# Scattering two sorted edge tables straight from the full index array, with the pieces of the first table divided anew over three stages

## The kernel before, in words

| phase | table | rounds | issued by |
|---|---|---|---|
| dst_in | src | 1 | L393 |
| dst_hist | src | 3 | L446 |
| dst_rank | src | 9 | L564 |
| proj0 | src | the rest, 4 | L1992 |
| up0 | dst | 3 | L1995 |
| proj1 | dst | the rest, 14 | L2017 |

## Time and profile before

### The profile page before, as it was taken

How to read it: one execution, slowest core, us unless ns; L and a number is a source line. 1 busy time by engine, 2 the same in 40 slices (tenths; PEclk the granted TensorE clock), 3 DMA queues, 4 the chain that set the end, 5 groups by cost and what they waited for, 6 DMA issues and landing times. The chain is left out here.

```text
span 6893.5 us, 55872 instructions
## 1 busy us (share of the span) xinstructions
PE 3674.6 (53%) x14811; PEld 2847.0 (41%) x14811; DVE 3431.6 (50%) x6662; ACT 1000.6 (15%) x2079; POOL 3392.8 (49%) x3358
## 2 busy tenths in 40 slices
PE   1373256662001455554666666685666659764542
PEld 1263155551001344443344444674454448333331
DVE  7594344443000444556677777446777762222225
ACT  0000122211000111111211111332111113210000
POOL 4787766668886455550254453004454410037662
PEclk9655567766555577776788887897888879886666
DMA  1142233441100233332455554115555530233333
GB/s 38 28 101 41 46 113 113 117 87 30 18 2 8 82 94 94 94 88 55 148 158 154 155 159 111 42 51 163 151 163 152 154 78 13 104 122 93 93 91 55
DMA packets 289794, 630.52 MB, mean 91 GB/s; under 512 B 79692, under 2 KB 134320, under 8 KB 286384
## 3 DMA queue, kind: packets, MB, share of 16 engines
q0 software_dynamic: 168256, 437.11, 25.6%
q1 hardware_dynamic: 121328, 190.89, 8.6%
HBM read 560.35 MB, written 66.48 MB: 91 GB/s over the span
## 5 line engine op out<-in xcount | busy, mean ns | idle before, releaser
L862 PE MATMUL edge_sums<-edge_rows,edge_hot 128*128 128x272 f32 (+3 forms) x4640 | 1518.4, 491 | 896.2 <-issue 241.3
L809 POOL DMA_INDIRECT edge_rows<-kv_rows,dst_index x928 | 879.8, 948 | 1547.7 <-POOLq L89 668.1
L862 PEld LDWEIGHTS edge_sums<-edge_rows,edge_hot 128*128 128x128 f32 x4640 | 1112.6, 248 | 1207.7 <-issue 411.1
L809 POOL DMA_INDIRECT edge_rows<-rel_rows,dst_other_index x464 | 466.4, 1005 | 755.3 <-ACTq L89 565.2
L1102 PE MATMUL edge_own_rows<-dst_x,edge_hot_t 128*128 x1856 | 615.6, 490 | 163.2 <-DVE edge_rows L936 118.4
L809 POOL DMA_INDIRECT edge_rows<-xl_rows,dst_index x464 | 457.9, 987 | 464.3 <-PE edge_sums L862 249.0
L809 POOL DMA_INDIRECT edge_rows<-rows,src_index x464 | 454.1, 979 | 235.5 <-issue 127.3
L1102 PEld LDWEIGHTS edge_own_rows<-dst_x,edge_hot_t 128*128 128x128 f32 x1856 | 442.6, 248 | 301.0 <-issue 220.5
L211 POOL DMA_INDIRECT table_dst<-proj_dst_put_stage x350 | 418.4, 1195 | 97.8 <-issue 86.2
L1019 DVE TENSOR_TENSOR edge_rows<-edge_rows,edge_turn_p 128x2048 f32<-128x2048 f32 x174 | 396.6, 2280 | 119.1 <-ACT edge_rows L1181 119.0
L872 DVE TENSOR_TENSOR l_acc<-l_acc,edge_sums 128x258 f32 (+1 forms) x464 | 197.9, 427 | 496.0 <-PE edge_sums L862 212.6
(11 more groups left out here) (389 smaller groups left out, 5386.5 us busy)
## 6 DMA issues: line engine op xcount, KB each, us to landing
edge_where<-local_dst SPq DMA_DIRECT2D x174, 256.0 KB
dst_rank_keys<-in_dst SPq DMA_DIRECT2D x85, 312.5 KB
rel_rows<-proj_out SPq DMA_DIRECT2D x25, 1024.0 KB
edge_where<-local_src SPq DMA_DIRECT2D x58, 256.0 KB
edge_rows<-kv_rows,dst_index POOLq DMA_INDIRECT x928
kv_rows<-proj_out SPq DMA_DIRECT2D x50, 260.0 KB, 2.0
edge_rows<-rows,src_index POOLq DMA_INDIRECT x464
edge_rows<-xl_rows,dst_index POOLq DMA_INDIRECT x464
```

The lines of the kernel that those rows point to most:

```text
L809: pool.indirect_dma_start(out=self.rows[:, h * U + b, 0:self.width], out_offset=None, in_=self.source[:, :], in_offset=bass.IndirectOffset ...
L862: last = nc.tensor.matmul(sums[p % len(sums)][:, 0:width], self.hot[s % 2][:, 2 * (p % 4) + i, :], self.half(s)[:, 2 * (p % 4) + i, first: ...
```

## The change

The staging buffers, their copies and the semaphore `staged` go. `piece` writes all its DMAs out, without a hardware loop, and each reads slot numbers and data from `stage_all` itself. The waits on `put[u]` now stand before the five DMAs of a group and ask for the group five back. The unused argument `ready` goes, and `stage_all` loses its last five columns, which only the copy read. The source table's rounds are divided 1, 4, 10 and the rest (2) over `dst_in`, `dst_hist`, `dst_rank` and `proj0`; those of the other table stay 3 and 14.

```diff
     def __init__(self, hold, tag, table):
         self.tag, self.table, self.next = tag, table, 0
-        self.stage_all = hold.sb(f"{tag}_stage_all", [EP, ET + LOOK, 5], i32)
+        self.stage_all = hold.sb(f"{tag}_stage_all", [EP, ET, 5], i32)
 
-    def piece(self, nc, ph, pool, n, ready=None):
+    def piece(self, nc, ph, pool, n):
         n = min(n, self.ROUNDS - self.next)
         if n < 1:
             return
-        first, table, stage_all = self.next * SLOTS, self.table, self.stage_all
+        put = [ph.sem(f"{self.tag}_put{u}") for u in range(SLOTS)]
+        for i in range(n):
+            for u in range(SLOTS):
+                after(pool, put[u], i * 16 * LOOK)
+                for j in range(LOOK):
+                    t = (self.next + i) * SLOTS * LOOK + u * LOOK + j
+                    pool.indirect_dma_start(
+                        out=self.table[:, :], out_offset=bass.IndirectOffsetOnAxis(ap=self.stage_all[:, t, 0:1], axis=0),
+                        in_=self.stage_all[:, t, 1:5], in_offset=None).then_inc(put[u], 16)
         self.next += n
-        stage = ph.sb(self.tag + "_put_stage", [EP, SLOTS, LOOK, 5], i32)
-        staged = ph.sem(self.tag + "_put_staged")
-        put = [ph.sem(f"{self.tag}_put{u}") for u in range(SLOTS)]
-        if ready:
-            pool.wait_ge(ready, 1)
-        nc.gpsimd.tensor_copy(stage[:, 0, :, :], stage_all[:, first * LOOK:(first + 1) * LOOK, :]).then_inc(staged, 1)
-
-        def body(i):
-            for u in range(SLOTS):
-                g, v = i * SLOTS + u, (u + 1) % SLOTS
-
-                after(pool, put[v], (i + (1 if v == 0 else 0)) * 16 * LOOK)
-                pool.wait_ge(staged, g + 1)
-                if ready and v == 0:
-                    pool.wait_ge(ready, i + 2)
-                nc.gpsimd.tensor_copy(stage[:, v, :, :],
-                                      stage_all[:, bass.ds((g + first + 1) * LOOK, LOOK), :]).then_inc(staged, 1)
-                for j in range(LOOK):
-                    pool.indirect_dma_start(
-                        out=table[:, :], out_offset=bass.IndirectOffsetOnAxis(ap=stage[:, u, j, 0:1], axis=0),
-                        in_=stage[:, u, j, 1:5], in_offset=None).then_inc(put[u], 16)
-
-        rounds(pool, n, body)
         for u in range(SLOTS):
             pool.wait_ge(put[u], n * 16 * LOOK)
...
-                scatter_beside(nc, ph, block, (earlier, 3))
+                scatter_beside(nc, ph, block, (earlier, 4))
...
-            scatter_beside(nc, ph, block, (earlier, 9))
+            scatter_beside(nc, ph, block, (earlier, 10))
```

## The result

Over nine runs the changed kernel took 6873.18 us (median; 6861.37 to 6884.59), the kernel before, on the same chip, 6895.34 us (nine runs, 6890.48 to 6905.62). The ratio is 0.9969, with a 95% interval of 0.996 to 0.9978: 22 us or 0.3% less, where 17.3 us were forecast. The median lies just inside the forecast's own range (6873 to 6884 us). The profiled execution, at 6861.37 us (span 6859.6), is the lowest of the nine and 34 us under the one before; alone it would lie under the 6863 to 6891 us given for 8 cases in 10.

A forecast was written before the change was run, and what follows sets the result against it. POOL's queue of scatters was taken to end all six scattering phases. 157 copies at 0.108 us (17.0) plus 0.3 for the starts gave 17.3 us off 6895.29: 6878.0 us, own range 6873 to 6884, 8 in 10 6863 to 6891.

The forecast's parts named there:

- What bounds the kernel: All six phases with scatters: POOL's queue of scatters sets their end, with POOL-only tails of 19 to 457 us.
- The copies: Between groups of scatters: 157 of 164 copies give 0.108 us each by start-to-start spacing, 17.0 us.
- Rival A: All pieces: the copies' whole busy time of 46.8 us comes out, giving 6848 us; chance 0.04.
- The inherited hold: Dst_hist beside VectorE: the next scatter takes over five copies' wait, groups stay 14.5 us, gain 0.
- Rival B: Dst_hist: the scatter behind a removed copy is not held, 8.6 us more, 6869 us; chance 0.10.
- Dst_rank: 34 copies beside short VectorE operations, costed at 0.108 us each, 3.7 us; bounds 16 and 31 us.
- The starts: Head of dst_rank, proj0 and proj1: first scatter 0.1 us sooner without its copies, 0.3 us in all.
- The waits and the straight code: Between groups and in every piece: waits between scatters and written-out code without a loop both cost 0.
- rival C: Group edges: the gap is 0.4 us instead of 0.30, gain next to nothing, 6895 us; chance 0.15.
- Rival D: Pieces past their first round: straight code starves POOL, gaps up to 1.0 us, 6937 us; chance 0.06.
- The move: Two rounds leave proj0 (-74.6 us), one each to dst_hist and dst_rank (+37.3 each); sum 0.
- The margin: End of proj0: POOL stays last by only 2 us, with SP's last store and its landing next.

The follow-up runs named there:

- experiment 1: Kernel before with only the first table's rounds divided 1, 4, 10, 2, copies and loop kept: 6418.0 against 6414.44 us, ratio 1.0004.
- Experiment 6: Changed kernel without the landing wait ending unfinished pieces, and with 12 scatters put into three phases that had none: 6842.74 us, ratio 0.995 against the kernel before.
- experiment 8: Kernels before and after, both unchanged, run again on a third chip: 6877.96 and 6857.55 us, ratio 0.9971.
- runs 2 and 3: Kernel before (6414.44 us there) with its loop written out, copies kept: 6417.86 us; then scatters without copies, old numbers of rounds: 6396.35 us.
- experiment 4: Kernel before with a second, unread copy ahead of each copy between scatters: 6901.98 against 6880.08 us, ratio 1.0041.
- experiment 2: Kernel before with its scatter loop written out and its copies kept: 6417.86 us, ratio 1.0005.
- experiment 9: Changed kernel with 128 rows in each scatter instead of 125: 6994.8 us, ratio 1.0171 against the kernel before.

## Why the prediction was right, step by step

**What bounds the kernel.** That POOL's queue sets the end of the phases with scatters held for all six: every phase changed by what its queue changed, and the moved rounds showed up in full at both ends (table above, experiment 1). Experiment 6 shows the limit: take 9 us more out of proj0 and POOL is not last there any longer.

**The copies: right in mechanism and size.** The sum took 157 copies at 0.108 us. The quiet group fell by 7.575 - 7.457 = 0.118 us in the first pair, by 7.563 - 7.455 = 0.108 in the second (experiment 8) and by 7.563 - 7.466 = 0.097 on the first chip (runs 2 and 3). So 0.108 is the middle of what three pairs give. The six pieces together fell by 19.7, 18.2 and 17.0 us in the same pairs, where 17.0 was forecast. Rival A, the copies' 46.8 us of busy time, is refuted by the group itself, and once more by the second copy of experiment 4, at 0.13 us.

**The inherited hold: right.** In the first 75 us of dst_hist five scatters still take 14.5 us, one to each operation of VectorE, with or without a copy. In the timeline of after (start, duration) it reads:

```profile
178.25 2.42 DVE L453 TENSOR_TENSOR dst_hist_lo_hot<-dst_hist_low,all_ramp_b 125x2176 bf16<-125x2176 bf16 x1
179.02 2.71 POOL L197 DMA_INDIRECT table_src<-src_src_stage_all  x1 [0.30 <-issue]
...
181.09 2.41 DVE L453 TENSOR_TENSOR dst_hist_lo_hot<-dst_hist_low,all_ramp_b 125x2176 bf16<-125x2176 bf16 x1
182.03 2.53 POOL L197 DMA_INDIRECT table_src<-src_src_stage_all  x1 [0.30 <-issue]
```

The scatter that slipped through in 1.21 us behind a copy is gone; each now bears the wait, and a group keeps its 14.41 to 14.73 us against 14.43 to 14.75 before. Five copies of 1.83 to 1.89 us busy were worth 0.02 us each. Rival B's 8.6 us did not come. The scatter at 179.02 ends at 181.73, 1.06 us after VectorE's operation (180.67), as it did before. The Trainium skill, SBUF — State Buffer, "SBUF: two separate sides", has the two engines exclude each other for a whole instruction; that the number of scatters is one to an operation agrees with it.

**Dst_rank: the term mis-sized most.** Its 34 copies were taken at 0.108 us, as the middle between bounds far apart. While VectorE works a group there fell from 7.933 to 7.772 us, 0.16 per copy. Over the whole piece its 44 copies gave 37.3 - 31.2 = 6.1 us (5.6 on the first chip), where 44 x 0.108 = 4.8 was taken, 1.4 too little. The row of after (busy, mean ns; idle before) is that of the earlier trace rows without its copies; its stretch is 345 to 621 us:

```profile
L197 POOL DMA_INDIRECT table_src<-src_src_stage_all x177 | 221.3, 1250 | 74.0 <-issue 53.6 <-ACTq L89 20.4
```

The mean scatter is 1.250 us for 1.261. A copy was itself now and then longer beside VectorE (up to 0.34 us for 0.21), and that went with it; neither bound was approached.

**The starts: right where they can be read.** In dst_rank the first scatter now starts 0.78 us behind SP's first issue, where 0.87 stood and 0.76 was expected:

```profile
345.01 2.24 SPq L557 DMA_DIRECT2D dst_rank_keys<-in_dst  x5
...
345.79 1.19 POOL L197 DMA_INDIRECT table_src<-src_src_stage_all  x1 [20.40 <-ACTq L89]
```

**The waits and the straight code: cost nothing, as said.** The gap is 0.30 us across every group's edge, so rival C, with 0.4 there, is out. Rival D's starvation would have shown as gaps up to 1 us; the longest between two scatters of a piece is 0.31 in the changed kernel, and experiment 2 has the straight code without the change, at a ratio of 1.0005.

**The move, and what is late next.** Dst_hist +36.2, dst_rank +31.2, proj0 -77.4, all within the ranges given. It had been seen that POOL would stay last in proj0 only by a little: the last store of the others and the last scatter now lie near each other.

```profile
799.93 10.11 SPq L1374 DMA_DIRECT2D rows<-proj_out  x5
...
813.32 1.18 POOL L197 DMA_INDIRECT table_src<-src_src_stage_all  x1 [0.30 <-issue]
818.88 0.33 SPq L689 DMA_DIRECT2D srcload_raw<-table_src  x1
```

SP's last issue ends at 810.04 and the last scatter at 814.50, 4.5 us later, where the prediction's own figures have 749.5 - 744.06 = 5.4. The margin had been put at 2 us, because a landing was counted for the store and none for the scatter. Experiment 6 gives it by measurement: of 8.9 us taken off POOL there, 6.6 came. A third round moved, 37 us, would have put the store last.

**The rest.** Of the 3.5 us by which the end of proj1 beat the 17.3, 1.4 are dst_rank, 0.7 proj0 and 0.5 proj1, by the table. The rest lies between the pieces, where 1.1 us went and 0.3 was forecast. Of these, 0.8 lie before the first scatter of all, which varies by more than that, and 1.2 between dst_hist and dst_rank; about 1 us comes back before proj0 and around edge0. The move alone (experiment 1 against 2) has those 1.2 us too (20.4 us for 21.6), and the prediction did not have them. The edge passes kept their length, apart from what they vary by themselves: 15.6 us of the profiled executions' difference is edge1's, and experiment 8 shows that it does not belong to the change. The medians' 22 us agree with the 20.8 and 21.3 us of the traces; that the median fell inside the range of 6873 to 6884 by only 0.2 us is luck, as its interval is some 6 us to either side.

## What to carry to other kernels

Price an instruction on POOL by the distance between the starts of its neighbours with it and without it, not by its span: 0.21 us of copy were worth 0.10 to 0.12, and 1.83 us of copy under a hold by VectorE were worth nothing. Take the distance from a place where the same waits stand between them. Before work is moved between phases ask which engine ends each of them; between two phases that the same queue ends it is neutral to about a microsecond in the traces, and only a phase (here dst_base, the weights, the read-back) where that queue stands idle outside of any ring gives a gain. A cheaper instruction on the queue that sets the end isn't a faster kernel until the others have been looked at beside it.

## What the runs showed of the hardware that had not been expected

- An indirect scatter of 128 rows costs POOL 0.96 us (median) where one of 125 rows costs 1.19. A stream of them, one every 1.26 us, brought the work of dst_rank nearly to a halt: VectorE 12 us busy in 100 for 92, traffic 14 GB/s for 100 (experiment 9; cause open).
- Two copies in a row on POOL start 0.15 us apart though each spans 0.21, and the second adds 0.13 us to the queue; with a wait for the first between them they start 0.27 apart.
- The change from dst_in to dst_hist costs POOL 3.4 us, and a landing of 2.6 us ahead of it adds only 1.3 (1.1 to 1.7 in four such places).
- Scatters take nearly the same time on all chips used here (proj1 529.4 to 530.9 us with one copy to a group), but edge passes do not: edge0 took 595 to 611 us on one chip and 664 to 673 on the others for the same gathers.
